# Two dense weight matrices and two biases are loaded behind the eighth instead of the last group of sorted attributes

## What is computed

```
x = x + L0(h, bases, w_comp, h_bias, edge_weight1, src, dst, edge_type)   # relational layer, 8 bases, 32 types
x = x + L1(h, W1, b1, W2, b2)                                             # two graph convolutions
x = x + L2(h, src, dst, edge_attr_20, edge_weight, edge_attr_4, ...)      # messages, one for each edge
x = x + L3(h, W1_l, W1_r, b1, W2_l, W2_r, b2)                             # two dense layers with a neighbour mean:
#   h = tanh(agg(h) @ W1_l.T + h @ W1_r.T + b1);  out = agg(h) @ W2_l.T + h @ W2_r.T + b2
```

## Time and profile before

| | us |
|---|---|
| median of three runs | 1456.11 (1455.35 to 1456.16) |
| the profiled execution | 1456.16 |
| its span, first to last instruction | 1454.3 |
| TensorE busy | 1364.6 (94%) |
| GpSimd busy | 892.1 (61%) |
| VectorE busy | 861.3 (59%) |
| ScalarE busy | 494.5 (34%) |

### The profile page before, as it was taken

How to read it: one execution, slowest core, us unless ns; L and a number is a source line. 1 busy time by engine, 2 the same in 40 slices (tenths; PEclk the granted TensorE clock), 3 DMA queues, 4 the chain that set the end, 5 groups by cost and what they waited for, 6 DMA issues and landing times. The chain is left out here.

```text
span 1454.3 us, 24122 instructions
## 1 busy us (share of the span) xinstructions
PE 1364.6 (94%) x6924; PEld 937.1 (64%) x6925; DVE 861.3 (59%) x2485; ACT 494.5 (34%) x1279; POOL 892.1 (61%) x927
## 2 busy tenths in 40 slices
PE   4888799999999999999999989998999979999998
PEld 2778788888885444444694866665666656686565
DVE  8778755555554667776433429988888854411111
ACT  7000000000005888882521235654555546311100
POOL 5777777777777777777777767777777720000000
PEclk9999999999999999999999989999999989999999
DMA  4678789888885652233211122222222330000000
GB/s 164 193 228 232 237 288 312 259 239 257 269 263 159 171 163 83 76 84 110 57 26 26 37 60 59 71 65 64 74 67 65 87 77 1 30 0 30 8 29 35
DMA packets 104166, 172.96 MB, mean 119 GB/s; under 512 B 20155, under 2 KB 54128, under 8 KB 104080
## 3 DMA queue, kind: packets, MB, share of 16 engines
q0 software_dynamic: 42832, 103.15, 24.2%
q10 hardware_dynamic: 27790, 39.30, 8.8%
q1 hardware_dynamic: 33458, 29.39, 6.5%
HBM read 153.74 MB, written 18.02 MB: 118 GB/s over the span
## 5 line engine op out<-in xcount | busy, mean ns | idle before, releaser
L874 POOL DMA_INDIRECT gath<-h_rows,idx x313 | 303.0, 968 | 95.0 <-issue 66.8
L1008 PEld LDWEIGHTS ps<-spread,gath 128*128 128x128 f32 x2504 | 306.9, 197 | 73.8 <-issue 43.4
L1008 PE MATMUL ps<-spread,gath 128*128 128x96 f32 x2504 | 313.0, 281 | 24.6 <-DMA gath<-h_rows,idx 17.7
L1030 PE MATMUL ps<-base_t,z 128*128 128x512 f32 (+1 forms) x640 | 308.4, 603 | 0.0
L930 POOL DMA_INDIRECT u<-u_rows,at x219 | 218.6, 998 | 66.8 <-issue 63.4
L1550 DVE TENSOR_TENSOR z<-z,ps 128x384 f32 x313 | 172.7, 552 | 100.1 <-PE ps L1008 88.5
L900 POOL DMA_INDIRECT slots<-att,idx_s x160 | 161.6, 1010 | 49.5 <-issue 47.6
L1221 PE MATMUL ps<-msg,hot 128*128 128x256 f32 x648 | 162.4, 394 | 20.6 <-DVE msg L1922 19.5
L900 POOL DMA_INDIRECT slots<-z,idx_s x153 | 153.5, 1003 | 43.9 <-issue 41.2
L1221 PEld LDWEIGHTS ps<-msg,hot 128*128 128x128 f32 x648 | 119.2, 192 | 81.0 <-DVE msg L1922 59.8
L1030 PEld LDWEIGHTS ps<-base_t,z 128*128 128x128 f32 (+1 forms) x640 | 107.3, 188 | 75.1 <-issue 74.9
(11 more groups left out here) (297 smaller groups left out, 1837.8 us busy)
## 6 DMA issues: line engine op xcount, KB each, us to landing
base_t<-in_bases_dram ACTq DMA_DIRECT2D x116, 256.0 KB
slots<-att SPq DMA_DIRECT2D x21, 256.0 KB, 5.2
at<-slots SPq DMA_DIRECT2D x21, 256.0 KB, 2.7
gath<-h_rows,idx POOLq DMA_INDIRECT x313, 4.2
u<-u_rows,at POOLq DMA_INDIRECT x219, 2.5
att<-in_attr_dram SPq DMA_DIRECT2D x40, 64.0 KB
slots<-att,idx_s POOLq DMA_INDIRECT x160
z<-in_attr_dram SPq DMA_DIRECT2D x39, 64.0 KB
```

The lines of the kernel that those rows point to most:

```text
L874: nc.gpsimd.indirect_dma_start(out=gath[:, c % RING, :], out_offset=None, in_=h_rows, in_offset=bass.IndirectOffsetOnAxis(ap=idx[:, par, c ...
L1008: last = mm(bank[:, k * SPREAD:(k + 1) * SPREAD], gath[:, h_slot, k * P:(k + 1) * P], s_of.rearrange("p b d -> p (b d)"), start=True, stop ...
L1030: return mm(ps[BANKS[n]][0:rows(n), :], z[:, k, b, n * P:n * P + rows(n)], base_t[:, k, :], start=(t == JOINS[n]), stop=(t == JOINS[n] + T ...
```

## The change

SyncE issues the four loads and the two waits ahead of them behind the first four pairs of groups, 0 to 7, in place of behind group 20 and the five small loads. The loop over the pairs is cut in two for this. No other engine's program changes, nor does any wait for the loads.

```diff
-            steps(sp, RADIALS // 2, 1, 0, sorted_pair, skip=1)
+            MIDDLE = 4
+            steps(sp, MIDDLE, 1, 0, sorted_pair, skip=1)
+            sp.wait_ge(out_ok, AGG[2])
+            sp.wait_ge(m_ok, RING)
+            for t, w in ((wa, s_w1l), (wb, s_w1r)):
+                sp.dma_start(t[:, :, :], w.rearrange("(k p) f -> p k f", p=P)).then_inc(ld_w3, 16)
+            sp.dma_start(b_a[:, 0:KIN], s_b1).then_inc(ld_w3, 16)
+            sp.dma_start(b_b[:, :], s_b2.to_broadcast([P, FEAT])).then_inc(ld_w3, 16)
+
+            steps(sp, RADIALS // 2, MIDDLE, 0, sorted_pair, skip=MIDDLE)
             sorted_quad(RADIALS - 1, 0)
             sp.wait_ge(u_ev, BLOCKS)
             ...
-
-            sp.wait_ge(out_ok, AGG[2])
-            sp.wait_ge(m_ok, RING)
-            for t, w in ((wa, s_w1l), (wb, s_w1r)):
-                sp.dma_start(t[:, :, :], w.rearrange("(k p) f -> p k f", p=P)).then_inc(ld_w3, 16)
-            sp.dma_start(b_a[:, 0:KIN], s_b1).then_inc(ld_w3, 16)
-            sp.dma_start(b_b[:, :], s_b2.to_broadcast([P, FEAT])).then_inc(ld_w3, 16)
```

## The result

The changed kernel took 1459.54 us, the kernel before it on the same chips 1455.1 us (medians of 20 runs each): ratio 1.0026, 95% interval 1.0016 to 1.0035. By the ratio it is slower by 3.8 us (the two medians are 4.4 us apart), where 1452.9 us and 3.2 us less were forecast. The 20 times of the changed kernel fall into two groups, 8 from 1454.0 to 1457.9 and 12 from 1459.3 to 1463.0. The profiled execution is of the upper group: it took 1462.02 us with a span of 1460.2.

What follows compares the result with a forecast made beforehand. TensorE was 94% busy, the message stage ran at GpSimd's pace, and its end waited for gathers delayed by the four loads. Sum: 1456.16 - 3.20 + 0 = 1452.96, forecast 1452.9 us from the median 1456.11; range 1450.3 to 1456.5.

Steps and rivals of the forecast that it cites:

- (1): End of message stage: without the loads, step 80's lag (last gather's start to `vy`) falls from 5.88 to 2.68: gain 3.20 us.
- (2): Mid-stage: the loads set VectorE and TensorE back about 4.6 us from step 25, won back in 15 steps; cost 0.
- longer gathers eat the gain: Behind step 25: longer gathers while VectorE catches up lose 2.6 us on GpSimd, giving 1455.5 us; chance 0.27.
- (3): Earlier landing of the weights: TensorE needs them at L1287 only, over 30 us after the landing; gain or loss 0.
- (4): Behind the stage: the low granted clock from 1190 to 1197 may shift; bounds -1.5 and +1.5 us, value taken 0.
- the change doesn't remove the stall: End of stage: the stall comes from the last attributes and five small loads, which stay: 1456.1 us; chance 0.04.

Runs made afterwards that it cites:

- late_loads_3: Kernel before, with the four loads held until all 81 steps' messages are made; ratio 1.0002 to the kernel before.
- spread_pad_before_3: Kernel before, with the empty slots naming 128 different rows in place of row 0; ratio 1.0014 to the kernel before.
- stall_alone_3: Four loads held until all 81 steps' messages are made, plus an unread VectorE maximum ahead of step 25; ratio 1.0029 to the kernel before.
- spread pair: Empty slots naming 128 different rows: in the changed kernel 0.9994; in the kernel before with the loads behind all 81 steps 0.9985.
- early_loads_3: Changed kernel with the four loads issued earlier, behind group 3 (MIDDLE = 2); ratio 1.0014 to the kernel before.
- spread_pad_after_3: Changed kernel, with the empty slots naming 128 different rows in place of row 0; ratio 0.9994 to the kernel before.

## Why the prediction was wrong

- **The step that failed** is in (1): "What is late next at step 80 is the gather itself", with a lag of 2.68 us. That is the lag of a gather of 128 different rows; step 80's fetch one row 128 times and need 5.0 to 5.8 us where `vy` waits for them (late_loads_3, changed kernel). The stall at step 77 was read rightly (spread_pad_before_3: 6.51 us from the weights), but it hid a second delay of nearly its size behind it. Between the last gather and the last L1221 the changed kernel needs 8.98 us where it was 9.04, so the term of -3.20 us measured -0.06; with the loads behind the stage the time is 1.0002 (late_loads_3). Two delays of some 3 us side by side look like one, and removing either gained nothing in the time. The row was there: the earlier trace rows give 1171 to 1176 a DMA share of 0.60 at 44 GB/s, when the weights had landed. I used that row for its clock only.
- **The second step** is in (2), "Cost: 0". The lag came out as forecast (6.42 us at step 25; forecast 6.38) but began one step early (24, not 25), and it was gone at step 31, in 7 steps rather than 15. It went quickly because GpSimd lost time, the rival's mechanism with its price of 2.6 us. Measured: 2.0 to 4.3 us on GpSimd against profiles without a setback, and by the ratios 3.5 us (changed kernel against late_loads_3, 1.0026 - 1.0002) and 3.9 us (stall_alone_3 against late_loads_3), of which a part may be the clock behind the stage. The spread pair on different chips (0.9994 and 0.9985) gives only 1.3 us, within its intervals of some 2 us each. Where VectorE falls behind a GpSimd that sets the pace, that is not free, and the trace said so in steps 8 to 18.
- (3) held: nobody waited at L1287, with loads at 959, 1160 or 1179 (906 in early_loads_3).
- (4) The clock: the profile had 2.8 us more, outside the bound of 1.5, but it varies that much between kernels with the same end.
- The rival "longer gathers eat the gain" had the mechanism and 1455.5 us; with a gain of 0 in place of 3.2 it would have said 1458.7, and 1459.5 was measured. That the two agree so well is partly luck, as the 1459.5 may hold some of the clock's 2.8 us. The rival "the change doesn't remove the stall" was right that the end stays late and wrong in its cause: neither the small loads nor the attributes made it late (spread_pad_after_3 has them all and a lag of 2.65 us).
- The Trainium skill's rule in "SBUF — State Buffer", section "SBUF: two separate sides", weighed in the prediction (a VectorE operation in a two-port mode and GpSimd lock each other out of a shared port pair), points the way that the runs went. stall_alone_3 shows that the two engines are coupled. When a held gather is let go stands in the rows above; VectorE's operations during the one of 2.60 us are all TENSOR_TENSOR, and no run here shows which of them holds it, or that a port does.

## What to carry to other kernels

Before a stall's cause is taken away, look at the steps behind it for a second one of its own: a lag that doesn't fall although its cause is over can be the sign, and so is a DMA share that is high while few bytes move. In a pipeline paced by one engine a stall of its followers isn't free if they slow that engine when they catch up; measure it by holding the follower alone. And empty slots should point at different rows.

## What was not expected of the hardware

- A gather of 128 rows of 512 bytes that are all the same row keeps the DMA engines 0.90 busy for 41 GB/s (different rows: 0.17 for 49 GB/s) and lands some 3 us later.
- VectorE held for 3.9 us in mid-stage made single gathers on GpSimd 2.48 and 2.60 us long in place of 0.95, up to six steps later; the long gathers of all eight profiles (over 1.9 us, 38 of them) end 0.29 to 0.31 us behind the start of VectorE's last operation of a step.
- The granted clock was 0.63 in one profile and 0.85 in another over the 23 us behind nearly the same pauses of TensorE; the eight profiles differ by up to 2.9 us there.
